# Testing for a tile's end at every edge slot in a graph convolution with experts, and 32 instead of 30 tiles computed ahead

## What is computed

```python
n = layernorm(x)
h = x + segment_sum((n @ W)[src] * edge_weight, dst) + b        # 12500 x 256
n = layernorm(h)
r = softmax(mean(n) @ Wr + br)      # one routing vector for all tokens, capped by capacity, softmax again
top2 experts e, weights w = softmax(top 2 of r)
y = sum over the 2 experts: w_e * (gelu(n @ W1[e] + b1[e]) @ W2[e] + b2[e])
out = h + layernorm(y + n) * gamma + beta
```

## Time and profile before

| | |
|---|---|
| median of 3 runs | 3268.88 us (3258.56 to 3274.06) |
| span of the profiled execution | 2384.3 us |
| the profiled execution's own time | not recorded |
| busy PE, PEld, DVE, ACT, POOL | 2211.0, 1730.4, 1052.3, 1193.0, 1598.6 us |
| instructions | 41652 |

### The profile page before, as it was taken

The page is one execution under the profiler, slowest core; times in us unless marked ns, Lnnn a source line. Parts: engine busy times, 40 slices in busy tenths (PEclk is TensorE's granted clock), DMA queues, the critical chain, the costliest instruction groups (busy, mean ns, idle before and its releaser), DMA issues. The chain is left out here.

```text
span 2384.3 us, 41652 instructions
## 1 busy us (share of the span) xinstructions
PE 2211.0 (93%) x9949; PEld 1730.4 (73%) x9950; DVE 1052.3 (44%) x2924; ACT 1193.0 (50%) x3203; POOL 1598.6 (67%) x1626
## 2 busy tenths in 40 slices
PE   2488999899999999999999999999998999999998
PEld 1366777676776777777777777777776777999997
DVE  7883223232232223232322323232222235899999
ACT  3577667665665555545534343322324116656654
POOL 6777777777777777777777777777777772242341
PEclk9999999999999999999999999999999999999999
DMA  9955667665656665566656655656565554333422
GB/s 371 333 170 156 203 203 241 186 188 180 184 183 182 179 176 175 178 185 192 186 176 189 189 172 188 182 169 190 179 193 165 183 162 135 101 113 110 134 92 68
DMA packets 226740, 425.79 MB, mean 179 GB/s; under 512 B 36675, under 2 KB 134774, under 8 KB 226600
## 3 DMA queue, kind: packets, MB, share of 16 engines
q0 software_dynamic: 75008, 204.90, 28.6%
q1 hardware_dynamic: 151160, 217.12, 27.9%
q10 hardware_dynamic: 432, 2.40, 0.3%
HBM read 341.53 MB, written 82.75 MB: 178 GB/s over the span
## 5 line engine op out<-in xcount | busy, mean ns | idle before, releaser
L588 POOL DMA_INDIRECT G<-xr_d,SRC x1467 | 1391.7, 949 | 446.9 <-issue 302.5
L1087 DVE TENSOR_SCALAR OH<-CST,DL,WR 128x128 f32<-128x128 f32 x1563 | 569.2, 373 | 1271.0 <-PE ps L1451 1140.1
L1451 PE MATMUL ps<-G,OH 128*128 x3126 | 739.5, 389 | 78.7 <-DVE OH L1087 58.7
L1451 PEld LDWEIGHTS ps<-G,OH 128*128 128x128 f32 x3126 | 596.7, 194 | 224.8 <-issue 143.3
L1434 PE MATMUL ps<-W2u,H 128*128 128x256 f32 x1920 | 430.6, 382 | 6.8 <-issue 6.0
L1423 PE MATMUL ps<-YU,W1u 128*128 128x512 f32 (+1 forms) x1024 | 426.4, 569 | 9.7 <-ACT H L783 8.5
L1434 PEld LDWEIGHTS ps<-W2u,H 128*128 128x128 f32 x1920 | 362.7, 191 | 69.4 <-issue 20.8
L1423 PEld LDWEIGHTS ps<-YU,W1u 128*128 128x128 f32 x1024 | 195.1, 191 | 206.3 <-issue 184.9
L791 ACT ACTIVATE YE<-ps 128x512 f32<-128x512 f32 (+1 forms) x128 | 72.6, 569 | 442.2 <-PE ps L1434 442.1
L783 ACT ACTIVATE H<-ps,b1a 128x512 f32<-128x512 f32 (+1 forms) x256 | 168.6, 661 | 226.1 <-PE ps L1423 225.8
L612 POOL TENSOR_TENSOR ZR<-ZV,mhalf 128x4 f32<-128x4 f32 (+1 forms) x23 | 31.4, 1366 | 218.0 <-DVE ZV L1259 218.0
(11 more groups left out here) (221 smaller groups left out, 2395.8 us busy)
## 6 DMA issues: line engine op xcount, KB each, us to landing
W1u<-in_W SPq DMA_DIRECT2D x64, 512.0 KB
W2u<-in_W SPq DMA_DIRECT2D x64, 512.0 KB
y_d<-YE SPq DMA_DIRECT2D x56, 512.0 KB, 5.4
G<-xr_d,SRC POOLq DMA_INDIRECT x1467
x_d<-X SPq DMA_DIRECT2D x98, 128.0 KB
yt_d<-YT SPq DMA_DIRECT2D x98, 128.0 KB, 3.3
XR<-in_x SPq DMA_DIRECT2D x97, 128.0 KB, 3.2
XL<-x_d SPq DMA_DIRECT2D x24, 512.0 KB, 4.7
```

The source lines that it names most:

```text
L588: e.indirect_dma_start(out=G[0:rows(s), held(s), :], out_offset=None, in_=x if s < FRESH else xr_d, in_offset=bass.IndirectOffsetOnAxis(ap ...
L1087: e.tensor_scalar(OH[:, s % OHR, :], iota, DL[:, s:s + 1], WR[:, s + 1:s + 2], ALU.is_equal, ALU.mult).then_inc(s_oh, 1)
L1451: e.matmul(ps[:, 0, 0:D], OH[:, r, :], Gf[:, bass.ds(g + r * D, D)], start=False, stop=True, skip_group_check=True).then_inc(s_main, 1)
```

## The change

- `event` is called behind every slot instead of every second one. `begin` takes the one slot in which the tile ends again, not two; `OHX`, `OHT` and `XND` have one matrix or column in place of two, and ACT makes one. `THR` holds the first slot itself.
- Group 8 is the group of two tiles instead of group 0. The groups computed ahead have 32 tiles, all 64 units are full, and `by_size` goes. In the last stage group 8, the first of 17, has two tiles.
- The weight of a tile in `events()` is 0.8 x slots - 3.0 from tile 15 on, and all units count the same.
- POOL's gather waits for one slot less, `s - 62`.
- The warming products before the last stage (L1524) read both halves of the first group's `YTh`, two times 256 columns, and wait for both.

```diff
-SMALL = 2
-NG = (NT - SMALL + GT - 1) // GT + 1
 AHEAD = 8
+SMALL = NT - AHEAD * GT - (NT - AHEAD * GT) // GT * GT
+SIZES = [GT] * AHEAD + [SMALL] + [GT] * ((NT - AHEAD * GT) // GT)
+STARTS = [sum(SIZES[:g]) for g in range(len(SIZES))]
+NG = len(SIZES)
...
-    room = [max(0.0, 0.75 * slots[t] - 3.5) * most[t] if t >= 14 else 0.0 for t in range(NT)]
-    size = [len(tiles(k // E)) / GT for k in range(UNITS)] + [1.0]
+    room = [max(0.0, 0.8 * slots[t] - 3.0) * most[t] if t >= 15 else 0.0 for t in range(NT)]
...
-                    e.wait_ge(s_main, s - RING + 3)
+                    e.wait_ge(s_main, s - RING + 2)
...
-                for k in range(2):
-                    step(e.activation(OHT[:, 0, k, :], iota, ACT.Abs, bias=XND[:, k:k + 1]))
+                step(e.activation(OHT[:, 0, :], iota, ACT.Abs, bias=XND[:, 0:1]))
                 e.wait_ge(s_act, chain)
-                step(e.activation(OHT[:, 1, :, :], OHT[:, 0, :, :], ACT.Relu, bias=ones[:, 0:1], scale=-1.0))
+                step(e.activation(OHT[:, 1, :], OHT[:, 0, :], ACT.Relu, bias=ones[:, 0:1], scale=-1.0))
...
-                e.wait_ge(s_main, odd + 1)
+                e.wait_ge(s_main, cut + 1)
                 if t:
                     e.wait_ge(s_begin, t)
                 e.wait_ge(s_act, chain)
-                for k in range(2):
-                    e.activation(OHX[:, k, :], OHT[:, 1, k, :], ACT.Copy, scale=WR[:, bass.ds(odd + k, 1)]).then_inc(s_ohx, 1)
+                e.activation(OHX[:, :], OHT[:, 1, :], ACT.Copy, scale=WR[:, bass.ds(cut + 1, 1)]).then_inc(s_ohx, 1)
...
-            e.tensor_scalar(THR[0:1, 0:NT - 1], FROW[0:1, 1:NT], 1, None, ALU.bitwise_or).then_inc(s_tab, 1)
+            e.tensor_copy(THR[0:1, 0:NT - 1], FROW[0:1, 1:NT]).then_inc(s_tab, 1)
...
-                e.matmul(ps[:, 0, 0:D], OHX[:, 0, :], Gf[:, bass.ds(g, D)], start=True, stop=False, skip_group_check=True)
-                e.matmul(ps[:, 0, 0:D], OHX[:, 1, :], Gf[:, bass.ds(g + D, D)], start=False, stop=True, skip_group_check=True).then_inc(s_begin, 1)
+                e.matmul(ps[:, 0, 0:D], OHX[:, :], Gf[:, bass.ds(g, D)], start=True, stop=True, skip_group_check=True).then_inc(s_begin, 1)
...
-            def by_size(do):
-                u = e.snap(u_r, min_val=0, max_val=UNITS - 1)
-                with e.If(u < E):
-                    do(u, SMALL)
-                with e.Else():
-                    do(u, GT)
...
-                            begin(e.snap(v_r, min_val=1, max_val=FINAL), g + (r - 1) * D)
+                            begin(e.snap(v_r, min_val=1, max_val=FINAL), g + r * D)
...
                     edge(g, r)
-                    if r % 2 == 1:
-                        event(a, r, g)
+                    event(a, r, g)
...
-                    e.matmul(ps[:, 7, :], ones_r[:, :], YTh[:, 0, 0, :], start=True, stop=True, skip_group_check=True)
+                    e.matmul(ps[:, 7, :].rearrange("p (c n) -> p c n", c=2), ones_r[:, :], YTh[:, 0, :, 0:SMALL * P], start=True, stop=True, skip_group_check=True)
...
-            e.wait_ge(s_yth, 1)
+            e.wait_ge(s_yth, 2)
...
-        "iota_e": (np.arange(NE) // 2 * 2).astype(np.float32)[None], "evt": evt,
+        "iota_e": np.arange(NE, dtype=np.float32)[None], "evt": evt,
```

More of the change, by code:

```diff
@@ L43, in group, with place_in @@
 def group(t):
-    return 0 if t < SMALL else (t - SMALL) // GT + 1
+    return max(g for g in range(NG) if STARTS[g] <= t)
 def tiles(g):
-    a = SMALL + (g - 1) * GT
-    return range(a, min(a + GT, NT)) if g else range(SMALL)
+    return range(STARTS[g], STARTS[g] + SIZES[g])
+def place_in(t):
+    return t - STARTS[group(t)]
 def part(t):
-    return slice((t - SMALL) % GT, (t - SMALL) % GT + 1)
-def place_in(t):
-    return t - tiles(group(t))[0]
+    return slice(place_in(t), place_in(t) + 1)
 def slot(t):
@@ L87, in events @@
     most = [0.75 if t == NT - 1 else 1.0 for t in range(NT)]
-    room = [max(0.0, 0.75 * slots[t] - 3.5) * most[t] if t >= 14 else 0.0 for t in range(NT)]
-    size = [len(tiles(k // E)) / GT for k in range(UNITS)] + [1.0]
+    room = [max(0.0, 0.8 * slots[t] - 3.0) * most[t] if t >= 15 else 0.0 for t in range(NT)]
     free, u, out = 0.0, 0, []
     for t in range(NT):
-        free += room[t] * sum(size) / sum(room)
+        free += room[t] * (UNITS + 1) / sum(room)
         n = 0
-        while u + n <= UNITS and (free >= size[u + n] / 2 or t == NT - 1):
-            free -= size[u + n]
+        while u + n <= UNITS and (free >= 0.5 or t == NT - 1):
+            free -= 1.0
             n += 1
@@ L477, in _ @@
                             e.wait_ge(yt_st[t % 4], 16 * (t // 4 + 1))
-                        e.dma_start(YL0[:, :, :], yt_d[post[0], :, :, :]).then_inc(yl_in[0], 16)
+                        w = len(tiles(post[0])) * P
+                        e.dma_start(YL0[:, :, 0:w], yt_d[post[0], :, :, 0:w]).then_inc(yl_in[0], 16)
                     if n == GT + 2:
@@ L651, in match @@
                 e.load([row_r], THR[0:1, t - 1:t])
-                odd = e.snap(row_r, min_val=1, max_val=NE - 1)
-                step(e.activation(XND[:, :], ND[:, bass.ds(odd - 1, 2)], ACT.Identity, bias=t128_row[:, t:t + 1]))
+                cut = e.snap(row_r, min_val=0, max_val=NE - 1)
+                step(e.activation(XND[:, :], ND[:, bass.ds(cut, 1)], ACT.Identity, bias=t128_row[:, t:t + 1]))
                 e.wait_ge(s_act, chain)
-                for k in range(2):
-                    step(e.activation(OHT[:, 0, k, :], iota, ACT.Abs, bias=XND[:, k:k + 1]))
+                step(e.activation(OHT[:, 0, :], iota, ACT.Abs, bias=XND[:, 0:1]))
                 e.wait_ge(s_act, chain)
-                step(e.activation(OHT[:, 1, :, :], OHT[:, 0, :, :], ACT.Relu, bias=ones[:, 0:1], scale=-1.0))
+                step(e.activation(OHT[:, 1, :], OHT[:, 0, :], ACT.Relu, bias=ones[:, 0:1], scale=-1.0))
             def copy(v, t):
                 e.load([thr_r], THR[0:1, t:t + 1])
-                odd = e.snap(thr_r, min_val=1, max_val=NE - 1)
-                e.wait_ge(s_main, odd + 1)
+                cut = e.snap(thr_r, min_val=0, max_val=NE - 1)
+                e.wait_ge(s_main, cut + 1)
                 if t:
@@ L769, in section @@
                 if s["copy"] is not None and s["copy"] + 2 < NT:
-                    e.wait_ge(s_ohx, 2 * s["copy"] + 2)
+                    e.wait_ge(s_ohx, s["copy"] + 1)
                     match(s["copy"] + 2)
@@ L1422, in unit_up, with unit_down @@
                     for c in range(2):
-                        ins = e.matmul(ps[:, UP[i % 2], 0:m * P], W1u[:, c, i * P:(i + 1) * P], YU[:, c, 0:m * P], start=(c == 0), stop=(c == 1))
+                        ins = e.matmul(ps[:, UP[i % 2], :], W1u[:, c, i * P:(i + 1) * P], YU[:, c, :], start=(c == 0), stop=(c == 1))
                     ins.then_inc(s_up, 1)
-            def unit_down(u, m):
+            def unit_down(u):
                 e.wait_ge(w2_in, u * 16 + 16)
@@ L1430, in unit_down @@
                     e.wait_ge(s_ye, u * 2 + (p + 1))
-                    for h in range(m // 2):
-                        j = m - 1 - (m // 2 * p + h)
+                    for h in range(GT // 2):
+                        j = GT - 1 - (GT // 2 * p + h)
                         for i in range(4):
@@ L1468, in event @@
                         with e.If(now < DOWNS):
[L1469 removed]
+                            unit_up(e.snap(u_r, min_val=0, max_val=UNITS - 1))
                     with e.Else():
```

15 lines of the change are left out of this document (7 added, 8 removed).

## The result

The changed kernel takes 3321.2 us (median of four runs, 3304.1 to 3331.1), beside 3263.7 for the kernel before: a ratio of 1.0174 (1.0143 to 1.0206), 57 us slower. The prediction was +171. The sign was right, and 3321 lies in the range; the size was three times too large.

A forecast was written before the change was run, and what follows sets the result against it. PE's sequencer was to bound the edge stage: array 1749, exposed tests 282 and surviving idle gave +157 to +276 us, taken as +177. With -6 in the last stage that made +171, 3440 us; range 3300 to 3540.

The forecast's parts named there:

- 884.6 us lie around the span: Whole run: the 3268.9 us median exceeds the profiled 2384.3 us span by 884.6 us, taken as unchanged and outside it.
- Sum: PE's edge stage: +157 to +276 us by how much idle survives; +177 taken, last stage -6, total +171.
- rival C: Small loss: each added test costs only its records, 0.24 us; 3300 to 3350 us; chance 14%.
- The test, 0.36 us; 0.61 a slot: PE's sequencer, edge stage: a test costs 0.36 us, making a slot 0.61 us against 0.432 in the array.
- Exposed 282 us: Edge stage: sequencer time exceeding the array's by 4.4 us per cycle over 64 cycles, 282 us, partly swallowed by 157 idle.
- 1749 + 282 + 18: PE's edge-stage need if waits are all swallowed: array 1749, exposed sequencer 282, and 18 more; 2049 us, +157.
- One product pair less: Tile starts: saves 97 x 0.43 = 42 us of array, but nothing more against the exposed sequencer.
- 32 tiles ahead: Edge stage: eight half units become full, 55 us more array; array total 1749, 14 more than before.
- First lap +5: Loop's first lap: larger body brings one more code-loading stall, PE starts later, 5 us.
- Clock: Clock falls oftener because the array idles more (0.98 before), carrying the forecast over 3540; 7% together with Rival D.
- Rival A and B: Edge stage: A, tests hidden, only last stage gains, 3263, 6%; B, also shorter last stage and fewer stalls, 3251, 6%.
- Rival D: Loop outgrows TensorE's instruction store: one 4.8 us stall in each of 195 laps, 936 us, about 4370; 7% with falling clock.

The follow-up runs named there:

- e1: Kernel before with one added ScalarE register operation at each tile end, profiled again; 3252.7 us, ratio 0.9999.
- e19: Kernel before without the gathers from slot 168 on or the waits for them; TensorE multiplies what lies in the ring; 2482.9 us.
- e17: e19 plus never-true tests with a body of one register move behind even slots; 2639.5 us.
- e18: The whole changed kernel without the gathers from slot 168 on; 2646.2 us.
- e13: Changed kernel again, with one added ScalarE register operation per tile end; ratio 1.0172 to the kernel before.
- e7: e3 plus never-true tests behind even slots, each with the whole event body; ratio 1.0113 to the kernel before.
- e3: Kernel before with the change's group part alone: 32 tiles ahead, tests at every second slot, two slots taken twice; 3258.4 us, ratio 1.0028.
- e4: Kernel before with the change's slot part alone: test behind every slot, one slot taken twice at tile starts, 30 tiles ahead; 7455 us, ratio 2.291.
- e2: Kernel before with never-true tests behind even slots, each with the whole event body; 7528 us, ratio 2.314.

## Why the prediction was right and wrong

*"884.6 us lie around the span. I take them as unchanged and make the sum against the span."* This is the step that failed. 1.8 us lie around a span. The 884.6 were inside it: 826 of them in the edge stage (2718 us in e1, 1892 in the first profile). 586 are idle time (675 instead of 89 us), most of which goes when the gathers are left out and signals are prompt (117 in e19), and 240 are a longer busy time (2043 instead of 1803), at a clock of 0.87 instead of 0.98. So the step "Sum", which let only some of 157 us idle be swallowed, had several times too little to swallow. The size of the loss depends on the idle time that the tests can hide in, and I had read that from an execution that had almost none. Without gathers, in a state like the first profile's, the change costs 163 us against my 171. That the measured time still lies in the stated range is luck: the range reached down to 3300 for the sake of a cheaper test (rival C), not of more idle time.

*The test, 0.36 us; 0.61 a slot.* Right: 0.604 in the last laps, 1732 tests.

*Exposed 282 us, less what of 157 idle is swallowed: +177.* Right in form. e17 measures 157 for the tests. In the timed state there was far more idle to swallow, and 25 us are left. The rule that waits are used up first was mine; the amount of waits was wrong. Of the 18 in "1749 + 282 + 18" only the 5 of the first lap have a source.

*One product pair less: worth nothing more against the exposed sequencer.* With prompt signals the sum that holds its saving of array comes out (e18 over e17, 7 us for 8). In the timed state it was too kind: e13 against e7 shows a loss of 19 us.

*32 tiles ahead: 55 us more array, +14 with the one-slot start, last stage -6.* Right with prompt signals, where e18 lies 7 us over e17. In the timed state the 55 were hidden: e3 is +9, where 55 less 6 would be 49. The last stage runs from the first product on YTh, at 2862.0 in e1 and 2923.9 in the changed kernel, to the end: 397.6 and 391.2 us, 6.4 less.

*First lap +5.* The first edge comes at 134.9 instead of 134.0 and the longest branch lasts 3.4 us. The first lap has five transfers of code where the kernel before has four, which is the one more that I had named; its time is too small to tell.

*Clock.* In the forecast only as a rival's aside. The granted clock over the edge stage is 0.87 in e1 and in the changed kernel, 0.98 where signals are prompt.

*Rival A and B* fell: a slot does cost the sequencer more than the array. *Rival C* named 3300 to 3350, which is where the time lies, but for a test of 0.24 us; its mechanism is refuted by the 4.83 us lap. *Rival D* didn't occur here, since 1254 instructions fit; with the slot part alone it did (e4), and by 4200 us, where I had priced one stall a lap at 936: a lap there fetches about ten times, not once.

## What to carry to other kernels

Hold a profile's span against a timed run before using it: if they are a quarter apart, the profile shows another kind of execution, and every estimate of what is hidden and what is exposed is made for the wrong one. Added sequencer work is paid only beyond the idle time that its engine has between events, so measure that idle time in the state that is timed. In a loop with unrolled bodies count the engine's instructions first: at 1582 (by my count) TensorE ran without fetches after the first lap, at 1902 every lap fetched ten blocks and the kernel took 2.3 times as long.

## What the hardware did that I had not expected

In the edge stage of e1 semaphore updates by TensorE reached VectorE and ScalarE up to 14 us after the record of the product while GpSimd issued gathers: 555 us of "remote" waiting before and behind the one-hots in e1, 1.4 us without gathers, 580 with a quarter of the rows. In the setup, gathers under way too, VectorE took up a result of TensorE at 50.2 whose last product's record ends at 31.4. The updates also came in bunches: the trace of the first profile has 43,636 records of semaphore updates, that of e2 40,363, that of e1 only 16,667, and for the gathers' own semaphores, which each gather raises by 16, 24,883 in the first profile and 5,116 in e1. Whether the others were merged on the way or only not recorded is open. The last stage, without gathers, takes 398 us in e1 and 397 in the first profile.

Removing 1395 gathers from a kernel that is not bound by them made it 23.5% faster, with TensorE's clock rising from 0.87 to 0.97 over the edge stage.

A loop of 1935 TensorE instructions by my count was fetched again in every lap, ten transfers of 16.4 KB, each of which goes with 2.2 us of added time ((7528 - 3252) / 1943).
